# Both seams of the first expert layer: its first two units made in the attention before it, the next attention's first tiles and key units made inside it

## The reference

```python
x = x + _L0_xattn_ref(_layernorm(x), ctx_2048, ...)
# experts: 32 of width 96, the 8 best of each token with their shares
logits = x @ gate_weight.T                      # of layernorm(x)
probs = softmax(logits); topv, topi = top_k(probs, 8)
...                                             # shares under 0.05 dropped
gu = x @ w_gu.T; g, u = split(gu)
acc = acc + (silu(g) * u) @ w_d.T * c_e[:, None]
# second attention, context first
k = rms_norm(ctx @ ki_w + ki_b, nki_s); v = ctx @ vi_w + vi_b
q = rms_norm(layernorm(x) @ q_w + q_b, nq_s)
out = softmax(q k.T / sqrt(128)) v; x = x + out @ o_w + o_b
```

## Time and profile before

| | |
|---|---|
| time, median of 3 runs | 1616.31 us (1615.84 to 1623.88) |
| profiled execution, time | 1618.3 us |
| its span | 1616.5 us |
| mean granted clock of TensorE | 0.974 |
| TensorE busy | 1487.2 us, 92% |
| VectorE, ScalarE, GpSimd busy | 904.2, 748.6, 527.4 us |
| first attention | to about 489.7 us |
| experts | to about 768.2 us |
| second attention | to about 1113.0 us |

### The profile page before, as it was taken

One profiled execution on the slowest core, in us unless ns is written; L12 is line 12 of the kernel. 1 busy time (PEld: TensorE's weight loads), 2 busy tenths in 40 slices (PEclk: granted clock), 3 DMA queues, 4 the chain that ended last, 5 costly groups with the idle time before them and its releaser, 6 DMA issues. The chain is left out here.

```text
span 1616.5 us, 22228 instructions
## 1 busy us (share of the span) xinstructions
PE 1487.2 (92%) x6990; PEld 1047.3 (65%) x6992; DVE 904.2 (56%) x1990; ACT 748.6 (46%) x2053; POOL 527.4 (33%) x511
## 2 busy tenths in 40 slices
PE   3989998899988999999999999998967999999998
PEld 1667776777764555556777979776734666654555
DVE  7787889888863342323454554554683555552321
ACT  3778787788871211110343435343463555552110
POOL 2566567877760000000433424221101333320000
PEclk8999999999997999999999999999987999999999
DMA  4201000200008100000100000002211000000000
GB/s 189 81 35 56 8 4 1 80 1 1 2 1 326 56 0 1 0 0 0 63 1 1 1 1 16 12 1 100 119 68 45 1 1 1 1 1 1 0 13 14
DMA packets 9717, 52.67 MB, mean 33 GB/s; under 512 B 1670, under 2 KB 3846, under 8 KB 6529
## 3 DMA queue, kind: packets, MB, share of 16 engines
q1 hardware_dynamic: 9008, 50.42, 8.1%
q0 software_dynamic: 160, 0.68, 0.2%
q10 hardware_dynamic: 432, 0.15, 0.0%
HBM read 50.87 MB, written 1.05 MB: 32 GB/s over the span
## 5 line engine op out<-in xcount | busy, mean ns | idle before, releaser
L1087 ACT ACTIVATE l0f_silu<-bank 128x512 f32<-128x512 f32 x48 | 28.7, 597 | 203.0 <-PE bank L1027 203.0
L1202 DVE TENSOR_TENSOR l0f_hidden<-l0f_product,bank 128x512 f32<-128x512 f32 x48 | 33.0, 687 | 155.3 <-PE bank L1038 155.3
L767 POOL TENSOR_TENSOR l0a_stepped<-l0a_y,l0a_m 128x512 f32<-128x512 bf16 x64 | 76.2, 1191 | 106.6 <-DVE l0a_m L569 106.2
L789 POOL TENSOR_TENSOR l0a_head_rstd<-l0a_head_var,all_minus_half 128x4 f32<-128x4 f32 x96 | 102.4, 1071 | 12.8 <-DVE l0a_head_var L588 12.7
L2127 PE MATMUL bank<-l3a_f_xn_t,all_weights_b 128*128 128x512 f32 (+1 forms) x208 | 94.0, 594 | 1.7 <-DVE all_weights_a L2310 1.7
L720 ACT ACTIVATE l0a_work<-bank,l0a_neg_max 128x128 f32<-128x128 f32 x256 | 90.5, 370 | 5.1 <-DVE l0a_neg_max L601 4.9
L1027 PE MATMUL bank<-l0f_xn_t,all_weights_b 128*128 128x512 f32 x192 | 91.9, 602 | 0.0
L187 POOL TENSOR_TENSOR l1a_l1a_norm_rstd<-l1a_l1a_norm_var,all_minus_half 128x8 f32<-128x8 f32 x1 | 1.6, 1633 | 275.4 <-DVE l1a_l1a_norm_var L173 275.4
L1583 DVE TENSOR_TENSOR all_weights_a<-bank,all_cols 128x512 f32<-128x512 f32 x64 | 44.0, 690 | 83.5 <-PE bank L1430 83.4
L1049 PE MATMUL bank<-all_weights_a,l0f_hidden 128*128 128x256 f32 x384 | 90.5, 378 | 0.0
L1027 PE MATMUL bank<-l0f_xn_t,all_weights_a 128*128 128x512 f32 x192 | 90.2, 592 | 0.0
(11 more groups left out here) (403 smaller groups left out, 3831.8 us busy)
## 6 DMA issues: line engine op xcount, KB each, us to landing
all_weights_a<-in_l_w_q SPq DMA_DIRECT2D x2, 2048.0 KB, 15.1
all_weights_b<-in_l_e_gate SPq DMA_DIRECT2D x1, 3072.0 KB, 10.6
all_weights_a<-in_l_e_up SPq DMA_DIRECT2D x4, 768.0 KB, 9.5
all_weights_a<-in_l_e_down SPq DMA_DIRECT2D x1, 3072.0 KB, 18.3
all_weights_b<-in_l_w_qx SPq DMA_DIRECT2D x1, 2048.0 KB, 11.4
all_weights_b<-in_l_w_proj_x SPq DMA_DIRECT2D x1, 2048.0 KB, 17.7
all_weights_b<-in_l_w_proj SPq DMA_DIRECT2D x1, 2048.0 KB, 8.9
all_weights_b<-in_l_w_q SPq DMA_DIRECT2D x1, 2048.0 KB, 8.2
```

The lines of the kernel that those rows point to most:

```text
L767: done = g.tensor_tensor(stepped[:, 0:n], value, step, ALU.add)
L789: g.tensor_tensor(head_rstd[:, m % 2, :], head_var[:, m % 2, :], res.minus_half[:, 0:HU], ALU.pow)\
```

## The change

In the first attention, VectorE, POOL, TensorE and ScalarE also normalise and turn tiles 0 to 3 (`first_rows`, `first_rstd`, `turn_first`, `keep_first`; the second pass over these tiles is finished four virtual tiles before). The rows lie in `wkx`, which is free by then, the turned tiles in `first_xn_t`, in region b. TensorE then makes the gate and up products of units 0 and 1 (`first_up`, four groups, one to a bank) between and behind the last output projections. For the first three units' up weights SP loads a small piece early, behind the gate weights. ScalarE ends the phase with a silu on one column.

The experts start with the routing logits and unit 2, `LAG` is 8, and all steps of the routing are moved by one. Their late tiles 4 to 7 are turned at steps 9 and 10. When the first half is added to `x`, its four tiles are normalised and turned for the next attention (`next_rows`, `turn_next`, `keep_next`, steps 35 to 38), into the same `first_xn_t`. Behind the last down product TensorE makes the first three key units of the next attention. There, tiles 4 to 7 are turned at steps 10 and 12 of the first period, and the class `TokenNorm` is gone.

```diff
+EARLY, FIRST_UP = 2, 3
+EARLY_KEYS = 3
...
+        F_TILE = VTS - 1
+        F_ROWS_TILE, F_ROWS = VTS - 2, [8, 11, 12]
+        F_TURN = [12, 13]
+        f_banks = (bank_of(F_TILE, NORMED[-2]), bank_of(F_TILE, PLAIN[-1]))
+        F_UP = [QUERY[-1] + 8, QUERY[-1] + 10, QUERY[-1] + 11, QUERY[-1] + 12]
+
+        def in_tile(tile, function, due):
+            def at_step(b, k):
+                if b == tile:
+                    function(k)
+            return at_step, due
...
+            def turn_first(k):
+                pe.wait_ge(f_rows_ready, 2 * k + 2)
+                if k == 0:
+                    norm_done.wait(pe, norm_done.at(F_TILE, NN - 1))
+                else:
+                    values_done.wait(pe, values_done.at(F_TILE, NV))
+                for i in range(2):
+                    for c in range(KC):
+                        at = (i * KC + c) * P
+                        mm = pe.transpose(f_banks[k][:, at:at + P], f_rows[:, 2 * k + i, c * P:(c + 1) * P], res.ident[:])
+                mm.then_inc(f_turned, 1)
+
+            def first_up(k):
+                if k == 0:
+                    norm_done.wait(pe, norm_done.at(VTS - 1, NN))
+                    values_done.wait(pe, values_done.at(VTS - 1, NV))
+                    turned_out.wait(pe, turned_out.at(VTS - 1, NN))
+                    pe.wait_ge(f_xn_ready, 2)
+                    pe.wait_ge(res.loaded["l0_e_gate"], 16)
+                    pe.wait_ge(res.first_up_loaded, 16)
+                n, up = divmod(k, 2)
+                weights = res.first_up if up else res.place["l0_e_gate"]
+                for c in range(KC):
+                    mm = pe.matmul(res.banks[2 * up + n][:], weights[:, c, n * P:(n + 1) * P], res.first_xn_t[:, c, :],
+                                   start=(c == 0), stop=(c == KC - 1))
+                mm.then_inc(res.first_up_made, 1)
+
             march(VTS, STEPS, [(turn_probs, later(at_query, 7)), (score, later(at_query, 4)),
-                               (mix, later(at_query, 8)), (project_out, later(at_query, 11)),
+                               (mix, later(at_query, 8)), in_tile(F_TILE, turn_first, F_TURN),
+                               in_tile(F_TILE, first_up, F_UP), (project_out, later(at_query, 11)),
...
+            def first_rows(k):
+                if k == 0:
+                    v.tensor_scalar(f_var[:], res.moments[:, 0:4, 1], EPS, None, ALU.add).then_inc(f_var_ready, 1)
+                    return
+                v.wait_ge(f_rstd_ready, 1)
+                for t in (2 * k - 2, 2 * k - 1):
+                    v.tensor_scalar(f_rows[:, t, :], res.x[:, t, :], res.moments[:, t, 0:1], f_rstd[:, t:t + 1],
+                                    ALU.subtract, ALU.mult).then_inc(f_rows_ready, 1)
...
-                               (round_mixed, later(at_query, 8)), (prepare, range(STEPS)), (quantise, [2, 4, 6])])
+                               (round_mixed, later(at_query, 8)), (prepare, range(STEPS)), (quantise, [2, 4, 6]),
+                               in_tile(F_ROWS_TILE, first_rows, F_ROWS)])
...
+            def keep_first(k):
+                act.wait_ge(f_turned, k + 1)
+                act.wait_ge(p_low, 2 * NA)
+                act.activation(res.first_xn_t[:, :, 2 * k * P:2 * (k + 1) * P].rearrange("p c (i n) -> p i c n", i=2),
+                               f_banks[k][:, :].rearrange("p (i c n) -> p i c n", i=2, c=KC), ACT.Copy)\
+                   .then_inc(f_xn_ready, 1)
...
+                               (swap_high, later(at_query, 2)), (swap_out_high, later(at_query, 11)),
+                               in_tile(F_TILE, keep_first, F_TURN)])
+            act.activation(q_t[:, 0:1], q_t[:, 0:1], ACT.Silu)
...
+            def first_rstd(_):
+                g.wait_ge(f_var_ready, 1)
+                g.tensor_tensor(f_rstd[:], f_var[:], res.minus_half[:, 0:4], ALU.pow).then_inc(f_rstd_ready, 1)
...
-def layer0_experts(nc, top, res, w, before):
+def layer0_experts(nc, top, res, w, bias, before):
 
 
     E, NCH, PARTS = 32, 24, 96
     HALVES, HALF = 2, 4 * P
     NF = HALVES * NCH
-    LAG = 7
+    LAG = 8
     DEEP = LAG + 1
     PIECES = 4
     TAU = 0.05
-    ROWS = [0, 1]
-    LOGITS = [0, 10]
-    SHIFT, SHARE, MEMBERS, SCALED, FALLBACK, ACTIVE, SPLIT = ([s, s + 11] for s in range(7))
-    TURN_WEIGHTS = [7, 18]
-    PAIRS = [8, 9]
+    ROWS = [2, 3]
+    LOGITS, KEPT = [0, 11], [1, 11]
+    SHIFT, SHARE, MEMBERS, SCALED, FALLBACK, ACTIVE, SPLIT = ([min(s + 1, 6), s + 12] for s in range(7))
+    TURN_WEIGHTS = [8, 19]
+    PAIRS = [9, 10]
+    NEXT_ROWS, NEXT = [NCH + LAG + 3, NCH + LAG + 4], [NCH + LAG + 5, NCH + LAG + 6]
+    LATE = 4
...
-            def turn_pair(p):
+            def turn_later(p):
...
-            def turn_later(i):
-                turn_pair(2 + i)
+            def turn_next(p):
+                pe.wait_ge(next_rows_ready, 2 * p + 2)
+                if p == 0:
+                    pe.wait_ge(weight_t_ready, 2)
+                else:
+                    pe.wait_ge(next_xn_ready, 1)
+                for i in range(2):
+                    for c in range(KC):
+                        at = (i * KC + c) * P
+                        mm = pe.transpose(late_bank[:, at:at + P], rows[:, 2 * p + i, c * P:(c + 1) * P], res.ident[:])
+                mm.then_inc(next_turned, 1)
...
             def up_products(n, _):
                 h, j = divmod(n, NCH)
-                if n == 0:
-                    pe.wait_ge(res.loaded["l0_e_gate"], 16)
-                if j == 0:
-                    pe.wait_ge(xn_ready, 2 * h + 2)
+                if n < EARLY:
+                    return
+                if h == 1 and j == 0:
+                    pe.wait_ge(xn_ready, 2)
                 product_done.wait(pe, product_done.at(n - 2, 1))
                 for bank, weights in ((gate_banks[n % 2], w_gate), (up_banks[n % 2], w_up)):
-                    if weights is w_up and h == 0 and j % (NCH // PIECES) == 0:
+                    if weights is w_up and n < FIRST_UP:
+                        weights = res.first_up
+                    elif weights is w_up and h == 0 and (j == FIRST_UP or j % (NCH // PIECES) == 0):
...
-            turn_pair(0)
-            turn_pair(1)
             march(NF, 1, [(once(LOGITS, gate_logits), [0]), (up_products, [0]), (once(TURN_WEIGHTS, turn_weights), [0]),
-                          (once(PAIRS, turn_later), [0]), (spread_weights, [LAG]), (down_products, [LAG + 1])])
+                          (once(PAIRS, turn_later), [0]), (spread_weights, [LAG]), (down_products, [LAG + 1]),
+                          (once(NEXT, turn_next), [0])])
+            product_done.wait(pe, product_done.at(NF - 1, 1))
+            pe.wait_ge(bias.ctx_loaded, 16)
+            pe.wait_ge(res.loaded["l1_w_k"], 16)
+            for u in range(EARLY_KEYS):
+                key_products(pe, res, bias.ctx_pairs[:, 0, :, :], u, res.banks[u]).then_inc(bias.keys_made, 1)
...
             def silu_of(n, _):
-                up_made.wait(act, up_made.at(n, 1))
+                if n < EARLY:
+                    act.wait_ge(res.first_up_made, 2 * n + 2)
+                up_made.wait(act, up_made.at(n - EARLY, 1))
                 product_done.wait(act, product_done.at(n - 2, 1))
                 act.activation(silu[:, n % 2, :], gate_banks[n % 2][:], ACT.Silu).then_inc(silu_done.sem, 1)
 
-            keep_pair(0)
-            keep_pair(1)
-            march(NF, 1, [(once(LOGITS, keep_logits), [0]), (once(SHIFT, exponentials), [0]), (silu_of, [0]),
-                          (once(TURN_WEIGHTS, keep_weights), [0]), (once(PAIRS, keep_later), [0])])
+            march(NF, 1, [(silu_of, [0]), (once(KEPT, keep_logits), [0]), (once(SHIFT, exponentials), [0]),
+                          (once(TURN_WEIGHTS, keep_weights), [0]), (once(PAIRS, keep_later), [0]),
+                          (once(NEXT, keep_next), [0])])
...
+                if h == 0:
+                    v.tensor_scalar(var[:], res.moments[:, 0:LATE, 1], 1e-5, None, ALU.add).then_inc(next_var_ready, 1)
+
+            def next_rows(p):
+                if p == 0:
+                    v.wait_ge(next_rstd_ready, 1)
+                    v.wait_ge(rows_turned, 2)
+                for t in (2 * p, 2 * p + 1):
+                    v.tensor_scalar(rows[:, t, :], res.x[:, t, :], res.moments[:, t, 0:1], rstd[:, t:t + 1],
+                                    ALU.subtract, ALU.mult).then_inc(next_rows_ready, 1)
...
+            g.dma_start(select[0:PARTS, :], w["l0f_select"]).then_inc(select_in, 16)
...
+def key_products(pe, res, ctx_t, u, bank):
+
+    for h in range(2):
+        for c in range(KC):
+            mm = pe.matmul(bank[:, h * 2 * P:(h + 1) * 2 * P], res.place["l1_w_k"][:, c, (2 * u + h) * P:(2 * u + h + 1) * P],
+                           ctx_t[:, c, :], start=(c == 0), stop=(c == KC - 1))
+    return mm
...
+                if p == PAIRS or ring_place(p, kind, u) < EARLY_KEYS:
+                    return
```

(7 more changed lines are left out.)

218 lines of the change are left out of this document (105 added, 113 removed).

## The result

| | before | changed |
|---|---|---|
| median of 8 runs each | 1621.64 us (1615.84 to 1625.09) | 1603.37 us (1600.18 to 1609.62) |
| ratio, 95% interval | | 0.9895 (0.9876 to 0.9915) |
| profiled execution: time, span | 1618.3, 1616.5 | 1604.07, 1602.3 |
| TensorE busy, granted clock | 1487.2, 0.974 | 1486.9, 0.975 |

The kernel is 1.05% faster, some 17 us (the interval of the ratio is 14 to 20 us). The forecast was 1596.6 (1592.5 to 1603.0): the direction is right, the time 0.4 us outside the range. The three first runs of the kernel before had a median of 1616.3; the eight have 1621.6.

A forecast was written before the change was run, and what follows sets the result against it. TensorE was taken as the bound, losing time idle or at its lower clock at two seams. 20.6 us gained by the fourth key unit, less 0.9 for late transposes, gave 19.7 less: 1596.6 us, range 1592.5 to 1603.

The forecast's parts named there:

- First seam: From first attention to experts: early units 0 and 1 fill TensorE's waits; unit 2 starts 13.9 us earlier.
- the last tile pays for everything: Rival: operations added to the attention's last tile lengthen its chain, 1.5 + 0.9 + 1.2 us more, 1600.2; chance 0.12.
- Switch: Block switch at the first seam: TensorE arrives last, at 491.2, and restarts 1.1 us later, at 492.3 to 492.4.
- Logits: Routing logits, first after the restart in the experts: 1.7 us warm instead of 3.4 cold.
- Mark one: Start of unit 2 of the experts: moves from 507.97 to 494.1, 13.9 us.
- A stall at the taken branch: TensorE might wait openly for instruction fetch at both block switches, some tenths longer; trace neither shows nor excludes it.
- Second seam: From experts to next attention: key units take 5.2 us before the barrier; fourth starts at 759.4 instead of 780.04.
- The rival on the slower side: Gate matmuls, logits and early products slow with both operands in one region; at 0.25 us each, 1626.6; chance 0.03.
- so a shift of these two marks reaches the end as it is: Earlier starts of unit 2 and the fourth key unit carry through, TensorE being all but gapless behind the second seam.
- So I take warm: First seam: clock assumed to stay up, the gap being 1.1 us with a filled stretch before it.
- the clock falls at the first seam all the same: Rival: logits 1.7 and a first unit up to 3.4 longer, 3 to 5 us in all, 1600.6; chance 0.13.
- The median of the runs is 1616.3, 2.0 lower: Base of the forecast: run median 2.0 us below the profiled 1618.3, so 1598.6 becomes 1596.6.

The follow-up runs named there:

- pow_late: Changed kernel with GpSimd's power for the first tiles moved one place later, behind the head's power; median 1601.13 us.
- after: The changed kernel, unedited, in its first profiled execution; 1604.07 us.
- keys2: Changed kernel with two key units instead of three ahead of the second barrier; median 1600.62 us, ratio to the kernel before 0.9874.
- cover: Changed kernel with 31 matmuls of 128x512, results overwritten, put into TensorE's waits behind the second attention; median 1597.68 us, ratio to before 0.9866.
- cover2: Changed kernel with two early key units instead of three and 58 filler matmuls of 128x256 in TensorE's waits; median 1591.62 us, ratio to before 0.9828.
- again: The changed kernel, unedited, executed again; median of 6 runs 1601.57 us, ratio to the kernel before 0.9885.
- seam1: Changed kernel keeping only the first seam's part, with the second attention and the experts' end as before; median 1604.72 us, ratio to before 0.9905.
- keys0: Changed kernel with no key unit ahead of the second barrier, all three behind it; median 1604.54 us.

## Why the prediction was right and wrong

**Right, term by term.** First seam: I had the fourth group starting 1.71 before 491.2 and TensorE ending there; it ended at 491.79. The last tile's second projection was 1.64 later than before (479.29 and 480.93), of which 0.41 had already been there ahead of the wait that GpSimd's power lengthened (440.38 and 440.79): 1.23, where I charged 1.1 for the power. By pow_late the power made 1.0 of it. Further on TensorE has a second new wait of 0.83 at 458.84, ahead of which VectorE made two of the added rows in 1.57 us; most of it is made good by the second projection. So 0.2 or so of the rival "the last tile pays for everything" is in it. Switch: 1.07 idle against 1.1. Logits: 1.78 against 1.7. Mark one: 494.64 against 494.1. A stall at the taken branch, as the Trainium skill (Runtime: NRT & Kernel Launch, Instruction fetch mechanics) has it, would have shown as a longer switch than the 1.1 us that I took; at 1.07 us nothing of it is seen. ScalarE's two table loads took 1.28 us each and its silu of unit 2 still waited 0.32 for TensorE. The Trainium skill (ScalarE: Activation LUTs, What ACT_TABLE_LOAD costs) has 2.66 us for a switch with its drain. The trace does not agree: both switches with the exponential between them took 2.9 us, from 495.14 to 498.04.

Inside: the wait ahead of the transposes of the routing weights is 0.60 instead of the 1.19 that I left, and I charged 0.9 for the eight transposes. The last down product ends at 751.98 against 751.9; that it is so near is in part luck, since a start 0.5 too late and a wait 0.6 shorter cancel. Second seam: key units 5.2 from start to start, as I had said, fourth unit at 759.07 against 759.4, late transposes 0.88 against 0.9. The rival on the slower side, both operands from one region, is gone: gate matmuls take 594 ns on average with both operands there and 592 with one in the other region.

**Wrong, two steps.** The first is the sentence that the kernel is all but gapless behind the second seam, "so a shift of these two marks reaches the end as it is". The 40 us that I showed for it lie between the seams; behind the second, TensorE stood still for 48 of 820 us in that same trace, and its clock was at the lower level for 41. The marks' 20.1 did reach the end of the attention; behind it 5.9 us went to low clock in that execution, and 0.8 in the next. The same step is in "So I take warm": I treated the clock at a short gap as one thing or the other. I also misread the rows that I gave for it: at the first seam of the kernel before the clock fell at 485.5, some 1.5 us into the wait of 2.31, not behind it. Of the eight executions that have the new first seam with early units, four kept the clock and four lost it about where unit 2 starts (after, keys2, cover, cover2; again, seam1, keys0, pow_late); a fall cost 1.7 us in the one where two traces of one kernel can be compared. At the second seam one cost 1.7 as well. My rival "the clock falls at the first seam all the same" had 0.13 and 3 to 5 us; it should have been about one half, and 1.7.

The second is the base: "The median of the runs is 1616.3, 2.0 lower". Of 66 executions of the kernel before in all, the median is 1619.2, and they lie in four heaps, near 1616, 1619, 1624 and 1627.5. A median of three at 1616.3 is a low draw: 6 in 100 triples out of these are as low. From 1619.2 the same sum gives 1599.5; the changed kernel's 14 runs have a median of 1602.5. The range's upper edge, 1603.0, stood on mechanisms only and held nothing for the kernels' own spread, 10 us for the changed one and 13 for the one before.

That leaves 16.7 us between the medians of all executions of each kernel, against 19.7. Falls behind the two seams, which the sum left out, explain roughly half of the missing 3: by these few traces half of 1.7 and a third of 1.7, 1.4 in all. The rest is within the intervals and stays open.

## What to carry to other kernels

Where one core runs with short waits, read two executions of the same kernel before blaming a change for what happens behind it: lay equal matmuls on each other, see where the lead changes, and look at the granted clock there. Price a gap of 1 to 3 us as a chance of a fall, not as surely at the high or the low clock, and take the base from as many runs as there are heaps. Work put ahead of a barrier should end when the slowest other engine arrives: the third key unit was one too many. And if the clock falls in waits that cannot be filled with work, fill them with matmuls that nobody reads, a little shorter than the wait.

## What the runs showed of the hardware

- The same program took 1615.4 to 1628.6 us, always on one core, in steps, with mean granted clocks of 0.980 to 0.967. Another chip did not change that: on three chips its medians were 1619.1, 1619.3 and 1618.9.
- The clock fell behind waits as short as 1.06 us with small matmuls behind them (the changed kernel's second execution), and behind two of 1.20 and 0.77 us in the middle of otherwise full work (533 in before's second execution), not in every execution.
- 58 matmuls without a purpose, some 25 us of TensorE's time, made the kernel before 6.6 us faster (1618.9 to 1612.2), and with two early keys the changed one 10.9 (1602.5 to 1591.6).
- From TensorE's last matmul to the restart of the engines a barrier took 0.93 to 1.07 us where TensorE came last (both seams of the changed kernel, keys2).
